# Message passing and a routed FFN on one core: the rows of turn 31 placed by one-hot products in the closing sums

## What is computed

```python
scores = sigmoid(xt @ Wg.T + bg)              # 64 experts
w, idx = top_k(scores, 2)                     # each row (token) goes to 2 of 64
w = w / w.sum(-1, keepdims=True)
cw = zeros((T, E)).at[arange(T)[:, None], idx].add(w)
nx = (xt - mu) * rsqrt(var + EPS)
h1 = nx @ (gamma * W1) + b1p                  # per expert, 512 -> 256
h3 = nx @ (gamma * W3) + b3p
hw = silu(h1) * h3 * cw.T[:, :, None]
y = einsum('eth,ehd->td', hw, W2) + cw @ b2   # per expert, 256 -> 512
z = shared expert of 32 hidden columns
x = x + y + z
```

## Time and profile before

| | before |
|---|---|
| median of three runs | 426.47 us |
| the profiled execution | 428.25 us |
| its span | 426.5 us |
| TensorE busy | 393.4 us, 92% |
| VectorE busy | 213.0 us, 50% |
| ScalarE busy | 156.6 us, 37% |
| GpSimd busy | 174.0 us, 41% |
| moved by DMA | 129.15 MB, mean 303 GB/s |

### The profile page before, as it was taken

One profiled execution on the slowest core, in us unless ns is written; L12 is line 12 of the kernel. 1 busy time (PEld: TensorE's weight loads), 2 busy tenths in 40 slices (PEclk: granted clock), 3 DMA queues, 4 the chain that ended last, 5 costly groups with the idle time before them and its releaser, 6 DMA issues.

```text
span 426.5 us, 6393 instructions
## 1 busy us (share of the span) xinstructions
PE 393.4 (92%) x1892; PEld 204.6 (48%) x1893; DVE 213.0 (50%) x698; ACT 156.6 (37%) x388; POOL 174.0 (41%) x276
## 2 busy tenths in 40 slices
PE   6988999999999998999999999999988968888985
PEld 4556777755656556443443444444433433334332
DVE  8899999225666677644324324233242232224346
ACT  8777788322332231232332332322321321223232
POOL 2769997313655576613423223223131132111100
PEclk9999999999999999999999999999999999989999
DMA  7999971400001745499999999999999999999978
GB/s 238 234 329 409 405 269 80 138 33 26 25 25 37 310 189 182 121 369 411 402 404 405 408 407 406 405 408 405 406 406 410 410 405 408 405 406 409 365 284 320
DMA packets 44022, 129.15 MB, mean 303 GB/s; under 512 B 7746, under 2 KB 8962, under 8 KB 43858
## 3 DMA queue, kind: packets, MB, share of 16 engines
q1 hardware_dynamic: 38242, 120.45, 74.2%
q0 software_dynamic: 5744, 8.28, 5.4%
HBM read 119.64 MB, written 17.85 MB: 322 GB/s over the span
## 4 chain that ended last, share of the span: by engine, by line
PE 77%; issue 6%; DVE 6%; DMA 4%; POOL 4%; SPq 1%; ACT 0%; DVEq 0%; POOLq 0%; ACTq 0%
PE bank L1516 27%; PE bank L1379 13%; PE bank L1548 13%; PE bank L1538 5%; PE bank L1328 4%; PE bank L1504 4%; PE bank L1301 3%; DMA w<-totals 2%; PE bank L1367 2%; PE bank L1400 2%; POOL AT L510 1%; POOL M L510 1%; PE bank L1388 1%; DVE stats L835 1%; PE bank L1523 1%
## 5 line engine op out<-in xcount | busy, mean ns | idle before, releaser
L1160 DVE SCALAR_TENSOR_TENSOR osl<-bank,b13T,osl 128x64 f32<-128x64 f32 x128 | 27.6, 277 | 151.0 <-ACT osl L755 145.9
L1516 PE MATMUL bank<-w,xhT 128*64 128x512 f32 x368 | 84.3, 598 | 10.0 <-issue 8.9
L748 ACT COPY xh<-bank 128x512 f32<-128x512 f32 x33 | 19.3, 585 | 133.8 <-PE bank L1516 130.8
L1379 PE MATMUL bank<-HW,AT 128*128 128x512 f32 x128 | 58.2, 592 | 0.0
L1516 PEld LDWEIGHTS bank<-w,xhT 128*64 128x64 f32 x368 | 25.7, 136 | 52.8 <-issue 49.1
L606 POOL DMA_INDIRECT totals<-GW,A x16 | 16.4, 1024 | 78.6 <-PE bank L1504 65.2
L606 POOL DMA_INDIRECT totals<-osl,A x16 | 16.4, 1027 | 76.8 <-PE bank L1504 66.3
L1548 PE MATMUL bank<-w,osl 128*64 128x512 f32 x184 | 44.0, 594 | 0.5 <-DVE osl L1160 0.5
L602 POOL DMA_INDIRECT A<-nx_rows,A x33 | 34.0, 1030 | 12.1 <-issue 9.6
L1379 PEld LDWEIGHTS bank<-HW,AT 128*128 128x128 f32 x128 | 22.9, 191 | 21.0 <-issue 21.0
L655 ACT ACTIVATE osl<-iota,eT 128x128 f32<-128x128 f32 x90 | 27.8, 387 | 9.9 <-PE bank L1328 9.9
(11 more groups left out here) (244 smaller groups left out, 587.2 us busy)
## 6 DMA issues: line engine op xcount, KB each, us to landing
w<-in_L_ffn_W_dram SPq DMA_DIRECT2D x69, 1024.0 KB, 19.6
A<-in_L_ffn_W_dram SPq DMA_DIRECT2D x15, 1024.0 KB, 19.1
HW<-in_L_ffn_W_dram SPq DMA_DIRECT2D x8, 1024.0 KB, 18.9
totals<-w SPq DMA_DIRECT2D x1, 4096.0 KB, 26.0
AT<-in_L_ffn_W_dram SPq DMA_DIRECT2D x4, 1024.0 KB, 19.8
w<-totals SPq DMA_DIRECT2D x8, 512.0 KB, 7.5
out_dram<-X SPq DMA_DIRECT2D x8, 256.0 KB, 4.1
X<-in_x_dram SPq DMA_DIRECT2D x3, 512.0 KB, 8.9
```

What stands on the lines that cost most here:

```text
L1160: ins = v.scalar_tensor_tensor(hT[b][:, m, CAP * h:CAP * h + CAP], bank[4][:, (HC + m) * P + CAP * h:(HC + m) * P + CAP * h + CAP], b13T[: ...
L1379: ins = t.matmul(bank[4 + s % 2][:, :], AT[:, s % 2, k, :], HW[:, k, :], start=(k == 0), stop=(k == NB - 1))
L1516: ins = t.matmul(bank[2 + b][CAP * h:CAP * h + CAP, :], xe[b][:, c, CAP * h:CAP * h + CAP], up_w[v][:, h, :, c, :], start=(c == 0), stop=( ...
```

## The change

Turn 31 is treated like turn 32: it isn't scattered, its rows stay in ysb[3], eight more placement matrices are built and one more gather of shares is made. SP waits for the scatters up to turn 30. TensorE places the rows of turn 31 in eight products more: blocks 0 to 3 ahead of turn 32's result (block 0 before turn 32's hidden rows are turned, blocks 1 and 2 behind that in place of three of seven spare transposes, block 3 behind down(32)), blocks 4 to 7 within the closing sums. BY_PE is now blocks 2, 3, 4 and 7, each with the half of back that TensorE adds; blocks 2 and 3 are added ahead of the wait for turn 32's result. ScalarE fills the banks of blocks 4 to 7 only. VectorE's adds and the banks are dealt out anew, and blocks are finished in the order 0 to 7.

```diff
-PLACE_ORDER = (0, 1, 2, 7, 3, 4, 5, 6)
-WHOLE = (0, 7)
-BY_PE = (4, 5)
+PLACED = (LAST - 1, LAST)
+AHEAD_OF_LAST = (0, 1, 2, 3)
+BY_PE = {2: 0, 3: 0, 4: 1, 7: 1}
...
+        place_at = lambda i: w2[:, RING - 2 + i // 8, (i // 4) % 2, P * (i % 4):P * (i % 4) + P]
+        place_rows = {turn: [place_at(NB * n + i) for i in range(NB)] for n, turn in enumerate(PLACED)}
+        share_diag = {i: A[:, SLOT_W + P * n:SLOT_W + P * n + P] for n, i in enumerate(BY_PE)}
...
-        last_bank = [bank[i] for i in (4, 1, 3, 5, 7, 0, 2, 6)]
+        last_bank = [bank[i] for i in (1, 5, 7, 4, 3, 0, 2, 6)]
...
             for i in range(YS):
                 if i != XS:
-                    sp.wait_ge(y_out[i], 16 * (LAST // YS))
+                    sp.wait_ge(y_out[i], 16 * sum(j % YS == i for j in range(PLACED[0])))
...
-            for n, s in enumerate((0, 1, 2, 3, 4, 7, 5, 6)):
-                sp.wait_ge(x_final, n + 1)
+            for s in range(NB):
+                sp.wait_ge(x_final, s + 1)
...
-                    pool.wait_ge(share_at_ready, 1)
-                    g.indirect_dma_start(wsh, None, shares, bass.IndirectOffsetOnAxis(ap=share_at, axis=0),
-                                         bounds_check=2 * N - 1, oob_is_err=False).then_inc(wsh_in, 16)
-                if j < LAST:
+                    pool.wait_ge(share_at_ready, 2)
+                    for turn in PLACED:
+                        g.indirect_dma_start(turn_share[turn], None, shares, bass.IndirectOffsetOnAxis(ap=share_at[turn], axis=0),
+                                             bounds_check=2 * N - 1, oob_is_err=False).then_inc(wsh_in, 16)
+                if j not in PLACED:
                     pool.wait_ge(y_ready, j + 1)
...
-            for i in range(NB):
-                if i in WHOLE:
-                    continue
+            for i in range(len(AHEAD_OF_LAST), NB):
+                if i == NB - 1:
+                    act.wait_ge(y_ready, R2 + LAST)
+                    hold(act)
                 act.wait_ge(back_in[i], 16)
                 a.activation(last_bank[i][:, :], back[i][:, 0, :], ACT.Identity, scale=share[:, i, 1:2]).then_inc(bank_filled, 1)
...
+                for turn in PLACED:
+                    d, at = DST[:, pair_of(turn):pair_of(turn) + 1], share_at[turn]
...
                 if j == LAST - 1:
+                    dve.wait_ge(wsh_in, 32)
+                    for turn in PLACED:
+                        link(v.tensor_copy(tokf, TOK[:, pair_of(turn):pair_of(turn) + 1]))
+                        link(v.tensor_scalar(token_at, iota[:, 0:NB], -float(P), tokf, ALU.mult, ALU.add))
+                        for i in range(NB):
+                            ins = v.tensor_scalar(place_rows[turn][i], iota[:, :], token_at[:, i:i + 1], turn_share[turn], ALU.is_equal, ALU.mult)
+                        ins.then_inc(last_places, 1)
+                    for i, k in BY_PE.items():
+                        ins = v.tensor_scalar(share_diag[i], ident[:, :], share[:, i, 1 - k:2 - k], None, ALU.mult)
                     ins.then_inc(last_places, 1)
...
+            c_0, c_1 = (mark(add_back(s, 0)) for s in range(2))
+            need(c_0)
+            c_0 = mark(add_back(0, 1))
+            need(c_1)
+            c_1 = mark(add_back(1, 1))
+            c_2 = mark(add_back(2, 1))
+            c_3 = mark(add_back(3, 1))
+            add_placed(0, c_0)
+            add_placed(1, c_1)
+            add_placed(2, c_2)
+            add_placed(3, c_3)
+            c_5 = mark(add_back(5, 1))
+            add_placed(4, c_5)
+            c_6 = mark(add_back(6, 1))
+            add_placed(5, c_5)
+            add_placed(6, c_6)
+            add_placed(7, c_6)
...
+            def place_turn(turn, i, start, stop=False):
+
+                return t.matmul(last_bank[i][:, :], place_rows[turn][i], ysb[turn % YS], start=start, stop=stop, skip_group_check=True)
...
+                if j == LAST:
+                    pe.wait_ge(last_places, 1)
+                    pe.wait_ge(y_ready, LAST)
+                    place_turn(LAST - 1, 0, start=True)
                 turn_hidden(j, j % 2)
-            keep_busy(bank[0], 7)
+            for i in AHEAD_OF_LAST[1:-1]:
+                place_turn(LAST - 1, i, start=True)
+            keep_busy(bank[0], 4)
             whole_bank(bank[0])
             down_of(PAIRS)
...
+            place_turn(LAST - 1, AHEAD_OF_LAST[-1], start=True)
+            for i in AHEAD_OF_LAST:
+                if i in BY_PE:
+                    pe.wait_ge(back_in[i], 16)
+                    add_total(i)
             pe.wait_ge(y_ready, R2 + LAST)
             hold(pe)
-            for i in PLACE_ORDER:
-                if i not in WHOLE:
-                    pe.wait_ge(bank_filled, i)
-                ins = t.matmul(last_bank[i][:, :], place_last[i], ysb[LAST % YS], start=i in WHOLE, stop=i not in BY_PE,
-                               skip_group_check=True)
-                if i in BY_PE:
-                    ins = t.matmul(last_bank[i][:, :], share_last[i], back[i][:, 1, :], start=False, stop=True, skip_group_check=True)
-                ins.then_inc(last_ps, 1)
+            for i in range(NB):
+                if i not in AHEAD_OF_LAST:
+                    pe.wait_ge(bank_filled, i - len(AHEAD_OF_LAST) + 1)
+                    place_turn(LAST - 1, i, start=False)
+                    if i in BY_PE:
+                        add_total(i)
+                place_turn(LAST, i, start=False, stop=True).then_inc(last_ps, 1)
```

More of the change, by code:

```diff
@@ L210, in moe_gnn @@
         zero_tile = w13[:, RING - 1, 0, :, :].rearrange("p c h -> p (c h)")[:, 0:D]
[L211 to L214, removed]
+        place_at = lambda i: w2[:, RING - 2 + i // 8, (i // 4) % 2, P * (i % 4):P * (i % 4) + P]
+        place_rows = {turn: [place_at(NB * n + i) for i in range(NB)] for n, turn in enumerate(PLACED)}
+        share_diag = {i: A[:, SLOT_W + P * n:SLOT_W + P * n + P] for n, i in enumerate(BY_PE)}
+        tokf, token_at = small[:, 241:242], small[:, 244:252]
+        at_block, at_rank = (small[:, i:i + 1].bitcast(i32) for i in (243, 252))
+        turn_share = {turn: small[:, i:i + 1] for turn, i in zip(PLACED, (240, 253))}
+        share_at = {turn: small[:, i:i + 1].bitcast(i32) for turn, i in zip(PLACED, (242, 254))}
         mv1 = small[:, 0:16].rearrange("p (s a) -> p s a", a=2)
@@ L998, in _ @@
             dve.wait_ge(edges_ready, 2)
-            v.memset(wsh, 0.0)
+            for turn in PLACED:
+                v.memset(turn_share[turn], 0.0)
             for i in range(2):
@@ L1114, in over_table, with placed_shares @@
                 v.tensor_tensor(chunk, chunk, inside, ALU.mult).then_inc(chunk_ready, 1)
[L1116 to L1124, removed]
+            def placed_shares():
+                for turn in PLACED:
+                    d, at = DST[:, pair_of(turn):pair_of(turn) + 1], share_at[turn]
+                    mark(v.tensor_scalar(at_rank, d, 10, None, ALU.arith_shift_right))
+                    mark(v.tensor_scalar(at_block, d, 7, NB - 1, ALU.arith_shift_right, ALU.bitwise_and))
+                    link(v.tensor_scalar(at, d, P - 1, 4, ALU.bitwise_and, ALU.arith_shift_left))
+                    link(v.scalar_tensor_tensor(at, at_block, 2.0, at, ALU.mult, ALU.add))
+                    link(v.scalar_tensor_tensor(at, at_rank, -1.0, at, ALU.mult, ALU.add))
+                    v.tensor_scalar(at, at, 1.0, None, ALU.add).then_inc(share_at_ready, 1)
             def over_experts():
@@ L1188, in _ @@
                     over_experts()
-                    last_shares()
+                    placed_shares()
                 if j + 1 <= LAST and j + 1 != EX:
@@ L1233, in _, with add_back, add_placed @@
                     over_product(j, 0, at_t)
-            def add_back(s):
+            def add_back(s, k):
                 dve.wait_ge(back_in[s], 16)
[L1238 to L1263, removed]
+                return v.scalar_tensor_tensor(X[:, s, :], back[s][:, k, :], share[:, s, 1 - k:2 - k], X[:, s, :], ALU.mult, ALU.add)
+            def add_placed(s, *marks):
+                need(*marks)
+                dve.wait_ge(last_ps, s + 1)
+                v.tensor_tensor(X[:, s, :], X[:, s, :], last_bank[s][:, :], ALU.add).then_inc(x_final, 1)
+            c_0, c_1 = (mark(add_back(s, 0)) for s in range(2))
[15 more added lines that the diff above has]
+            add_placed(7, c_6)
         @block.tensor
@@ L1638, in _, with add_total @@
                     over_down(j, 0)
-            pe.wait_ge(last_places, 1)
+            pe.wait_ge(last_places, 3)
+            def add_total(i):
+                t.matmul(last_bank[i][:, :], share_diag[i], back[i][:, BY_PE[i], :], start=False, stop=False, skip_group_check=True)
+            place_turn(LAST - 1, AHEAD_OF_LAST[-1], start=True)
[3 more added lines that the diff above has]
+                    add_total(i)
             pe.wait_ge(y_ready, R2 + LAST)
             hold(pe)
-            for i in PLACE_ORDER:
```

(9 more changed lines are left out.)

## The result

The changed kernel takes 432.5 us (median of four runs, 432.08 to 433.62), the kernel before 427.02 us (median of four runs, 426.43 to 427.66). The ratio is 1.0117, with a 95% interval of 1.0087 to 1.0146: slower, by about 5 us (3.7 to 6.2; the medians as they stand are 5.5 apart). The forecast was 431.3 against 426.47, 4.8 more. The profiled execution took 432.54 us, its span is 430.8 us.

The account below looks back on a forecast made before the run. The prediction saw two bounds side by side, the read stream and TensorE's closing sums. Ten more products (8.6 us), less idle filled, transposes dropped and a shorter end, gave +4.8 us: 431.3, range 429.0 to 433.0.

Parts of the forecast that it names:

- The price of a product: TensorE's closing products: one fp32 matmul of 128x128 by 128x512 leaves two records 0.43 us apart, so takes 0.86 us.
- Sum: Whole span: ten more products are 8.6 us, partly filling idle time; +4.8 us taken on the span of 426.5.
- TensorE's second part: From turn 32's second products on: 17 products behind them instead of ten, TensorE ending at 427.85 with the tail.
- the unknowns: Turn 32's delay and the reads' start: no delay and no read waits give 430.2; full delay, reads no earlier, 431.9.
- rival C: Closing sums: TensorE falls to half clock for a stretch, costing 1.70 us more, 433.0; chance 8%.
- The delay of turn 32: Turn 32's second products on TensorE start 0.7 us late, at 410.95 instead of 410.23; bounds 0 and 0.8.
- The first product: Turn 31's product before turn 32's hidden rows are turned: 0.86 us, fitting TensorE's 0.69 us idle to within 0.1.
- The end behind the last add: From the last add's end to the end of the span: 2.77 us, kept as in the kernel before.
- Costs put at zero: Turn 1's second share addresses and gather, and VectorE's extra matrices in turn 31: covered by slack, no added time.
- Rival A: SP's wait before the eight reads: read-back sets the end, starts 0.5 to 3.8 us earlier, 426.0 to 422.7; chance 7%.
- Rival B: Gain and cost nearly cancel: products cost as forecast, but something that gets earlier sets the end, 426.5; chance 4%.
- D: Turn 32 isn't delayed and its reads wait nowhere: 430.2, inside the forecast's own range; forecast with it 81%.

Follow-up runs that it names:

- run 2: Kernel before with each of turn 32's eight placement products issued twice, nothing else of the change; ratio to the kernel before 1.0128.
- run 3: Changed kernel without the eight products that place turn 31, all else of the change kept; ratio to the kernel before 1.0023.
- run 5: Changed kernel with the four totals (blocks 2, 3, 4, 7) added by VectorE instead of TensorE; ratio to the kernel before 1.0021.
- run 7: Changed kernel with rows scaled, split into two bf16 parts and placed by 0/1 matrices in two bf16 products; ratio to the kernel before 0.9987.
- run 1: Kernel before with turn 31 left out of the output and the read-back waiting for turn 30's scatter; ratio to the kernel before 0.9992.
- run 4: Changed kernel with turn 31's products of blocks 1 and 2 moved behind turn 32's second products; ratio to the kernel before 1.0145.
- run 6: Changed kernel without four spare transposes and one spare product ahead of turn 32's second products; ratio to the kernel before 1.0094.
- run 8: As run 7, with block 7 placed first of the late blocks, its totals by VectorE, a block 6 total by TensorE; ratio to the kernel before 0.9983.
- run 9: As run 7, with blocks 0 and 1 placed before the totals of blocks 2 and 3, and no spare transposes; ratio to the kernel before 1.0014.

## Why the prediction was right

- **The price of a product, 0.86 us: right,** and what carried the forecast. Runs 2, 3 and 5 take it in three ways, read at TensorE's end (eight more: 6.7 us; eight fewer: 3.8, since waits come back; four fewer: 3.3). The rule that the prediction cites from the Trainium skill, TensorE: Matmul & The Clock Gate, section Step-by-step: what each phase is for, of one streamed column per cycle, doesn't hold for fp32 operands; with bf16 operands it does (0.215 us for 512 columns at a granted clock of 1.00, run 7). Four times that is the fp32 product, and another page of the Trainium skill, FP8 and Floating Point Precision, section TensorE Precision Notes, says just that: true FP32 takes four passes through the array.
- **Sum: right.** +4.8 forecast, +4.9 in the tail. By steps: the reads 0.5 us earlier (3.27 us into the tail instead of 3.80, so 0.53); TensorE's second part from 410.95 to 427.85, 16.9 us, measured 17.0 (410.52 to 427.52).
- **The absolute number was nearer to the edge than the sum.** 432.5 is 1.2 us above the 431.3, above the 430.2 to 431.9 that the unknowns were given, and 0.5 below the upper end of 433.0. That upper end was room for the half clock of rival C, which didn't come, so that it took in the measured time is luck. Of the 1.2 us, 0.55 are the base (426.47 of three runs, 427.02 of four), and the rest is that the medians lie 5.5 apart where the sum had 4.8; the ratio (5.0) and the tails (4.9) stand nearer to it.
- **Two steps were off a little and cancelled.** The delay of turn 32: 0.7 forecast, 0.9 measured (8.12 us into the tail against 7.22). The first product cost 0.2 instead of at most 0.1, since the turning of the hidden rows started 4.54 us into the tail instead of 4.34. The end behind the last add: 2.77 forecast, 2.48 measured (428.32 to 430.8). I had named the emptier queue as a reason for a longer range, and not put it into the sum.
- **Costs put at zero: borne out.** In turn 1, the second six operations ran (182.29 to 183.06) and the rows of turn 2 were ready at 184.48, 0.6 us ahead of the product at 185.11, as forecast. ScalarE's fills are done 2.4 us or more ahead of their use. The sixteen matrices and four diagonals end at 405.2, 3.5 us ahead of VectorE's next work.
- **Rival A: false in both its halves.** The start of the reads moved by 0.5 us, not 3.8 (run 1), and ten products don't fit into TensorE's slack. Turn 30's scatter landed 5.6 us after its issue in the changed kernel and in run 1; the 2.6 us that the prediction estimates by the fit of the Trainium skill, DMA: Bandwidth & Descriptors, section Anatomy of one DMA — SWDGE (gpsimd) path, doesn't hold beside the weight stream, and agrees only with turn 31's 2.4 us behind it.
- **Rival B** is out by the interval (1.0087 at least). **Rival C:** no half clock in the tail; the granted clock is 1.00 in each stretch above. **D**, that turn 32 isn't delayed, is wrong as a fact (0.9 us). Undoing the delay by moving products behind it gains nothing (run 4); undoing it by dropping spare work ahead of it takes 0.8 us off the tail (run 6).
- My own expectation of what comes next behind the products (the read of block 7) was wrong in runs 3 and 8 and missed by 0.07 us in run 7; in run 9 I took TensorE's queue for the bound and left out that the read of block 7 lay right behind it. The forecast for this change didn't rest on it.

## What to carry to other kernels

Where the chain of waits goes through one engine and another is full beside it, count the added work on the full one before counting what the chain may gain. Here the waits named the read-back, and TensorE, 1.1 us off that chain, took on 8.6 us of products, of which 6.1 came out at its end, for 0.5 us of earlier reads. Price products by the spacing of the starts in the trace at their own type, and compare tails of two traces from a common event, not from the start of the span. A queue that waits for one early transfer passes its idle to everything behind: look for that before naming the last transfer as the next bound. And when two bounds lie within a tenth of a microsecond, relieving one shows nothing.

## What was not expected of the hardware

Turns ahead of the closing sums ran at half clock in places, and not in the same ones. In the changed kernel it is turns 28 and 30 (first rows of TensorE's timeline below; turn 29 between them at full clock), before it was turn 29:

```profile
367.36 5.24 PE L1524 MATMUL bank<-A,xhT 128*64 128x512 f32 x16 [1.90 <-issue]
...
375.74 3.65 PE L1524 MATMUL bank<-HW,xhT 128*64 128x512 f32 x16 [0.26 <-issue]
...
384.00 5.35 PE L1524 MATMUL bank<-w,xhT 128*64 128x512 f32 x16 [1.73 <-issue]
```

Each comes after TensorE has idled 1.7 to 1.9 us and costs 1.6 to 1.7 us of that turn. The granted clock was 0.60 from 384.60 to 388.40, and 1.00 from 375.70 to 379.40. Such an idle alone doesn't bring it: turn 27 of the changed kernel started after 1.68 us of idle and turn 28 of run 3 after 1.90, both with full-clock products of 3.65 us.

The half-clock turns don't show in the start of turn 32, which waits for its weights in all these kernels. From turn 25's first product to turn 32's are 59.86 us in run 3, where none of these turns ran at half clock, 59.95 in the changed kernel and 59.89 in run 5, where two did, and 59.6 to 60.0 in all eleven kernels. So the spread of that start (401.3 to 403.7) is there by turn 25, which starts between 341.45 and 343.76. What makes it before that was not looked into.
